# Factorised field interactions with an MLP tower: ScalarE's sums go through a PSUM bank of their own, and the bank ring has six banks where it had seven

## The reference

```python
e = jnp.stack([tbl_0[ids[:, 0]], ..., tbl_39[ids[:, 39]]], axis=1)
p = e[:, rowidx]
q = e[:, colidx]
z = jnp.einsum('bie,fie,bif->bi', p, param, q)
h = jnp.concatenate([z, dense_ctx], axis=1)
h = jnp.maximum(h @ W_top1 + b_top1, 0.0)
h = jnp.maximum(h @ W_top2 + b_top2, 0.0)
y = h @ W_top3
```

## Time and profile before

| | |
|---|---|
| Time, median of 3 runs | 1218.11 us (1217.02 to 1220.1) |
| Span of the profiled execution | 1255.3 us |
| PE busy | 1224.6 us (98%) |
| DVE busy | 1053.7 us (84%) |
| ACT busy | 972.3 us (77%) |
| POOL busy | 573.2 us (46%) |
| HBM read | 80.09 MB, 64 GB/s over the span |

### The profile page before, as it was taken

How to read it: one execution, slowest core, us unless ns; L and a number is a source line. 1 busy time by engine, 2 the same in 40 slices (tenths; PEclk the granted TensorE clock), 3 DMA queues, 4 the chain that set the end, 5 groups by cost and what they waited for, 6 DMA issues and landing times.

```text
span 1255.3 us, 22898 instructions
## 1 busy us (share of the span) xinstructions
PE 1224.6 (98%) x5808; PEld 476.8 (38%) x5808; DVE 1053.7 (84%) x1720; ACT 972.3 (77%) x7177; POOL 573.2 (46%) x607
## 2 busy tenths in 40 slices
PE   6989999999999999999999999999999999999999
PEld 3323433333333333333333433334333334333333
DVE  6858899988888797889998888788999878899980
ACT  0019999975868887898968988799968988899951
POOL 5655554455455555555245555555245555400000
PEclk9988899999999999999999999999999999999999
DMA  7033344433544333333454433333353434122100
GB/s 207 18 113 104 79 119 117 110 104 92 140 100 120 102 104 87 88 81 97 106 134 106 113 84 94 87 80 96 95 155 90 114 97 111 49 63 83 44 1 1
DMA packets 132098, 118.87 MB, mean 95 GB/s; under 512 B 91351, under 2 KB 110039, under 8 KB 131965
## 3 DMA queue, kind: packets, MB, share of 16 engines
q1 hardware_dynamic: 111188, 94.94, 27.3%
q0 software_dynamic: 19200, 19.70, 7.6%
q10 hardware_dynamic: 1576, 2.76, 0.8%
HBM read 80.09 MB, written 0.01 MB: 64 GB/s over the span
## 4 chain that ended last, share of the span: by engine, by line
PE 88%; ACT 7%; issue 2%; DVE 2%; DMA 1%; SPq 0%; ACTq 0%; DVEq 0%
PE ring L793 40%; PE z_ps L816 18%; PE ring L798 17%; PE ring L822 8%; ACT wide_prod L606 6%; PE ring L756 2%; PE ring L826 2%; DVE prod L671 1%; DMA z_t<-tbl 1%; DVE wide_prod L685 0%; ACT e_t L567 0%; PE ring L774 0%; PE ring L829 0%; ACT h L620 0%; PE ring L767 0%
## 5 line engine op out<-in xcount | busy, mean ns | idle before, releaser
L606 ACT ACTIVATE wide_prod<-wide_prod 128x64 f32<-128x64 f32 x3520 | 841.8, 242 | 55.1 <-DVE wide_prod L685 34.8
L537 POOL DMA_INDIRECT rows<-tbl,idx_now x600 | 572.4, 954 | 514.9 <-DMA rows<-tbl,idx_now 310.0
L671 DVE TENSOR_TENSOR prod<-ring,e_t 128x512 f32<-128x512 f32 x1008 | 630.6, 683 | 114.3 <-PE ring L793 97.0
L606 ACT ACTIVATION_READ_ACCUMULATOR wide_prod<-wide_prod 128x1 f32 x3520 | 662.6, 188 | 17.8 <-issue 17.1
L793 PE MATMUL ring<-e_t,w 64*128 64x512 f32 x2176 | 584.3, 613 | 13.6 <-issue 4.8
L685 DVE TENSOR_TENSOR wide_prod<-ring,rows 128x512 f32<-128x512 f32 x512 | 327.8, 682 | 32.1 <-PE ring L798 12.8
L793 PEld LDWEIGHTS ring<-e_t,w 64*128 64x128 f32 x2176 | 229.0, 187 | 326.0 <-issue 210.0
L798 PE MATMUL ring<-w,e_t 64*128 64x512 f32 x1024 | 305.8, 616 | 4.2 <-DVE wide_prod L685 1.8
L816 PE MATMUL z_ps<-prod,strip 128*32 128x512 f32 x2096 | 253.9, 598 | 0.0
L798 PEld LDWEIGHTS ring<-w,e_t 64*128 64x128 f32 x1024 | 116.2, 189 | 150.5 <-issue 85.9
L816 PEld LDWEIGHTS z_ps<-prod,strip 128*32 128x32 f32 x2096 | 55.0, 109 | 179.7 <-issue 117.0
(11 more groups left out here) (24 smaller groups left out, 76.4 us busy)
## 6 DMA issues: line engine op xcount, KB each, us to landing
w<-weights SPq DMA_DIRECT2D x64, 768.0 KB
planes<-words SPq DMA_DIRECT2D x284, 64.0 KB
rows<-tbl,idx_now POOLq DMA_INDIRECT x600
z_t<-tbl SPq DMA_DIRECT2D x10, 224.0 KB
w<-weights SPq DMA_DIRECT2D x4, 512.0 KB
w<-hot_ids ACTq DMA_DIRECT2D x7, 256.0 KB
w<-w1z SPq DMA_DIRECT2D x7, 256.0 KB
words<-rows SPq DMA_TRANSPOSE x71
```

What stands on the lines that cost most here:

```text
L537: nc.gpsimd.indirect_dma_start(out=fields([tile], slice(slot, slot + 1), t)[:, 0, f, :], out_offset=None, in_=tables[m * 2 + f], in_offset ...
L606: last = nc.scalar.activation(products, products, ACT.Copy, accum_out=z_b[:, h, t, col:col + 1])
L671: nc.vector.tensor_tensor(dst[:, j, :], ring[:, bank, :], e_t[:, k, :], ALU.mult).then_inc(t_free, 1)
```

## The change

ScalarE's accumulator outputs go to a new PSUM tensor, `z_acc`, one bank of 4 x 128 columns, and no longer to `z_b` in SBUF. When the last wide item of a half has been summed, `keep_half` copies the columns that ScalarE has written from `z_acc` to `z_b`, one copy for each of the four batch tiles in which there are any (31 copies in all); columns of the wide items that DVE reduces are left out by a step in the pattern. The first sum of the next half waits for these copies (`half_kept`), the copies wait for the transposes that read `z_b` in the chunk before, and PE's transposes wait for `half_kept` and for DVE's reductions. PSUM has eight banks, `z_ps` and `z_acc` take one each, and `RING` goes from 7 to 6. Lags, step places and the order of the items are unchanged.

```diff
-RING = 7
+RING = 6
...
+def kept_columns(half):
+    c, h = divmod(half, HALVES)
+    rows_in = P // WIDE_PAIRS
+    for t in range(BT):
+        mine = [r for r in range(rows_in) if not reduced_by_vector(c, (h * rows_in + r) * BT + t)]
+        if mine:
+            step = mine[1] - mine[0]
+            assert mine == list(range(mine[0], mine[-1] + 1, step))
+            yield t, slice(mine[0], mine[-1] + 1, step)
...
+KEPT = [len(list(kept_columns(_h))) for _h in range(HALVES_ALL)]
...
         z_ps = ps("z_ps", [P, NB])
+        z_acc = ps("z_acc", [P, BT, P])
...
-                if v % (NW // HALVES) == 0 and c > 0:
-                    act.wait_ge(turned, (c - 1) * HALVES + h + 1)
+                if v % (NW // HALVES) == 0 and c * HALVES + h > 0:
+                    act.wait_ge(half_kept, sum(KEPT[:c * HALVES + h]))
                 act.wait_ge(t_free, through(PLACE[c, "wide", v]))
                 for jj in range(2):
                     for i in range(2 * FIXED):
                         products = wide_prod[:, slot, jj, E * i:E * i + E]
                         col = first + 2 * FIXED * jj + i
-                        last = nc.scalar.activation(products, products, ACT.Copy, accum_out=z_b[:, h, t, col:col + 1])
+                        last = nc.scalar.activation(products, products, ACT.Copy, accum_out=z_acc[:, t, col:col + 1])
                 last.then_inc(reduced_s, 1)
+
+            def keep_half(half):
+                c, h = divmod(half, HALVES)
+                wides = (half + 1) * (NW // HALVES)
+                by_vector = sum(reduced_by_vector(*divmod(v, NW)) for v in range(wides))
+                act.wait_ge(reduced_s, wides - by_vector)
+                if c > 0:
+                    act.wait_ge(turned, (c - 1) * HALVES + h + 1)
+                for t, own in kept_columns(half):
+                    nc.scalar.activation(z_b[:, h, t, :].rearrange("p (m w) -> p m w", w=WIDE_PAIRS)[:, own, :],
+                                         z_acc[:, t, :].rearrange("p (m w) -> p m w", w=WIDE_PAIRS)[:, own, :],
+                                         ACT.Copy).then_inc(half_kept, 1)
...
                         reduce(c, v)
+                    if v % (NW // HALVES) == NW // HALVES - 1:
+                        keep_half(c * HALVES + v // (NW // HALVES))
...
             def turn_half(half):
-                wait_reduced(pe, (half + 1) * (NW // HALVES))
+                pe.wait_ge(half_kept, sum(KEPT[:half + 1]))
+                pe.wait_ge(reduced_v, sum(reduced_by_vector(*divmod(v, NW)) for v in range((half + 1) * (NW // HALVES))))
```

More of the change, by code:

```diff
@@ L418, in bilinear_tower @@
         reduced_v = sem("reduced_v")
+        half_kept = sem("half_kept")
         turned = sem("turned")
```

## The result

The changed kernel takes 1254.99 us (median of 4 runs, 1254.14 to 1255.53) against 1218.16 us: it is 36.8 us slower, ratio 1.0273, 95% interval 1.0221 to 1.0325. The time is inside the range, the direction is as forecast, and the loss is nearly twice the 20 us forecast.

The account below looks back on a forecast made before the run. TensorE and VectorE, waiting for each other in turn through the short PSUM ring, were taken as the bound. Terms -3.2 - 0.9 + 0 + 10.8 + 13 = +19.7 us moved 1218.1 to 1238 us, range 1216 to 1262.

Parts of the forecast that it names:

- Part 1, sums into PSUM: ScalarE's accumulator reads into PSUM save 20 ns a pair, gaining 3.2 us in the stretch to 130 us.
- The 0.9 us behind L620: PE's two waits for the bank that ScalarE empties there, 0.9 us in all, counted as fully gained.
- Part 2, the copies: 31 ScalarE copies to SBUF at 290 ns, with waits under 2 us a half, hidden: 0 us.
- Part 3, six banks, the steps: At 18 MLP steps inside the chunks DVE idles one block, 0.60 us, longer each: +10.8 us.
- Part 3, the sums: DVE's 68 waits not at MLP steps grow with a bank less: 26 us, halved to +13 us.
- the 120 forecast: Sign in the new profile: DVE's waits for PE in 344 to 1240 us at 97 + 11 + 13, some 120 us.
- B: Rival: no change that can be told, later cycles taking back the MLP steps' cost; 1219 us, chance 0.12.
- C: Rival: faster, the PSUM write saving much more than 20 ns and the ring having a bank spare; about 1213 us, 0.08.
- E: Rival: the PSUM write is dearer, 20 ns more a pair, losing 3.2 us early; 1244 us, chance 0.03.
- D: Rival: much slower, all 68 waits growing (41 us) and some 6 us more for held banks; 1272 us, 0.10.
- A: The forecast itself: moderately slower, +4 to +46 us, from waits on both sides of the ring; chance 0.67.
- the further 6 us: Added cost in D: banks that steps and transposes hold until ScalarE copies them come round one block sooner.

Follow-up runs that it names:

- r1: The kernel before, unchanged, profiled a second time: 1225.65 us, profile span 1223.9 us.
- r2: The kernel before with six banks in the ring instead of seven and nothing else changed: 1260.56 us, ratio 1.033.
- r4: The kernel before, seven banks, with ScalarE making 13 of 16 sums of a tile, other columns zero: 1220.87 us, ratio 1.0017.
- r5: The changed kernel run again, without an edit: 1255.87 us, ratio 1.0294 to the kernel before.
- r3: The changed kernel with seven banks and sums straight to SBUF, keeping the copies (onto themselves) and their waits: 1222.24 us, ratio 1.0009.
- r6: The kernel before with five banks in the ring instead of seven: 1353.12 us, ratio 1.1092.
- r7: The kernel before with six banks and each group's sums issued in two parts of four blocks, two items apart: 1251.06 us, ratio 1.0254.
- r8: The kernel before with seven banks and each group's sums issued in two parts of four blocks, two items apart: 1239.54 us, ratio 1.0161.

## Why the prediction came out as it did

**Part 1, sums into PSUM.** Right in kind, too small in size: 42 ns a pair where I took 20, inside the bounds of 0 and 79. The profile should have shown the read at 167 ns; it shows a median of 264 (least 144), since durations now contain more than the work. The gain in the first chunk is 5.2 to 5.3 us by the profiles (I had 3.2); the slot waits that it removes are 4.2 us in r1 and r2, where the odd profile had 6.5. It is seen with six banks alone: with seven, r4, which stands in for it with fewer sums, gives nothing that can be told. The 0.9 us behind L620 belonged to the odd profile. Together some 5 us where I had 4.1. The estimate from the figures of the Trainium skill, page "ScalarE: Activation LUTs", section "What ACT_TABLE_LOAD costs", was 20 ns as well; the measurement, twice that, decides. The caveat on that page (section "Step-by-step: what each stage is for"), that PSUM as the destination is of use only where TensorE doesn't need most of it, agrees with r2 and r5: the bank costs 40.5 us and the shorter sums give some 5.

**Part 2, the copies.** Right: r3 is 1.0009, the 31 copies have a median of 277 ns (290 forecast) and start only 0.16 us apart, the first of them as little as 0.46 us after the start of the last sum, so that they cost less than I had, and PE has no wait for ScalarE between 344 and 1240 us in the changed kernel.

**Part 3, six banks, the steps.** Mis-sized, too large. "There are 12 and 6 such steps inside the chunks, and each should cost 0.60 us more: 18 x 0.60 = 10.8 us." At the step of the earlier trace rows it seemed to come true (3.23 to 3.83), but only against the odd execution; from r3 it is 3.50 to 3.83. Over all, the twelve long steps went from 46.0 or 46.4 to 49.1 us, and the six of eight instructions from 12.0 to 12.0: 3 us in all. Step by step (r3, r2, r6; each the same in all three chunks within 0.02 us) DVE's idle time shows why:

| items since the sums before the step | seven banks | six | five |
|---|---|---|---|
| 6 (second step, 14 instructions) | 3.26 | 3.86 | 4.46 |
| 5 (first step, 14) | 3.50 | 3.83 | 4.43 |
| 4 (third step, 14) | 4.72 | 4.83 | 5.55 |
| 4 (fourth step, 14) | 3.84 | 3.84 | 4.43 |
| 3 (fifth step, 8) | 1.60 | 1.60 | 1.85 |
| 4 (sixth step, 8) | 2.39 | 2.39 | 2.98 |

I had assumed that PE is at the ring's limit when a step begins. With seven banks it is only where six items have passed since the last sums, and half the way with five; after three or four it hasn't caught up with DVE, the seventh bank is empty, and its loss costs 0.11 us or nothing. The blocks that are issued and not finished by DVE when each of the six steps begins, in the order of the steps, bear it out: 5, 6, 5, 5, 4, 5 with seven banks (r3), 5, 5, 5, 5, 4, 5 with six and 4 each with five.

**Part 3, the sums.** This is the term that was too small. "I take half of that, 13 us: a bank lost in one cycle partly means that the next cycle begins nearer to the limit and loses less". It doesn't: cycles of one length lose the same, one after another (the table of cycles under r6), since PE comes back to the ring's limit before the next group and then has one block less issued. What lowers the loss is the length of the cycle, which I hadn't looked at. Measured is 54 less 22 or 26: 28 to 32 us, against 26 before I took the half, and 9 to 11 us more in chunk 0, which I hadn't counted at all. My upper bound for the sums, 41 us, holds for chunks 1 to 3. The way of counting was also led astray by the first profile: it showed 68 waits of DVE that were not at steps, where an ordinary execution of that kernel has 52. That DVE's waits in 344 to 1240 us came to 115.7, near the 120 forecast, confirms nothing for that reason: the growth is 26 us from the 89.4 of r1 and 32 from the 83.5 of r3, and the forecast counted from 97.2.

With measured sizes the terms are -5 for the faster sums, 0 for the copies, +3 and +1 for the steps, +30 for the groups, +10 for chunk 0, and -5 for waits that six banks end (the column "other" falls from 6 or 7 to 1.4 us; PE's waits for late tiles are gone in r2), together +34 us, against 37 timed. The rest is within what r1 and r3 differ by. In chunks 1 to 3 my errors largely cancel: 24 us forecast for steps and groups together, and some 29 measured, with the steps 8 us too much, the groups 17 too little and the 5 us of "other" not foreseen. Chunk 0, where I had 3 us gained and the changed kernel begins chunk 1 4 to 6 us later than r1 and r3, is the rest. That the time fell inside the range owes something to this luck.

**The rivals.** B fell with r2 (no cycle takes anything back), C with r4 and r2, E with the 197 ns. Its counterpart D, with every wait growing by a whole block, put the sums at 41 us and was nearer to the measured 28 to 32 than A's 13; what kept the time from 1272 us is mainly that the steps lost 3 us and not 10.8, and that the further 6 us don't show: in the changed kernel PE has no wait for ScalarE in 344 to 1240 us.

**Open.** What took ScalarE and others out of step in the first profile isn't known. That late tiles eat part of the gain of r4 was read, not tried. How much of the smaller worth of a bank in r7 and r8 is due to shorter bursts and how much to PE's added work is open. Other lags of the groups for six banks weren't tried.

## What to carry to other kernels

A ring between two engines of nearly equal speed should be measured against the longest common burst of the faster one's other work. Here DVE gets its first product behind a group of sums 3.1 us after the sums begin, with seven banks (893.31 to 896.39) as with six (915.79 to 918.88), and needs five products of 0.60 us in stock to bridge that. When the sums begin, it has five or six with seven banks, five with six and four with five, the one that it is working on among them. Below the need a cycle pays one consumer step for each bank taken away, but only where it is long enough for the producer to fill the ring again: shorter cycles keep the last bank empty and lose nothing with it. So the first bank (40 us) is cheaper than the second (93 us). Before counting waits in a profile, set its span beside the timed runs; where it is 3% longer, take another.

## What the runs showed of the hardware

An accumulator read of ScalarE into PSUM shortens the distance from one ACTIVATE with accumulation to the next from 239 to 197 ns (128x64 fp32), 18%. In that form the trace's durations no longer add up to time: they grow from one ACTIVATE to the next in an unbroken series, up to 818 ns, while most starts stay 197 ns apart.

Leaving the 64-row matmuls of the blocks for the 32-column ones of the sums, and coming back, costs TensorE 0.34 us (6.69 us for five items and a group in two parts in r8, 6.35 for the same work with the group in one in r1). In 130 more places it made the kernel 18 us slower where TensorE was nearly full (r8).
